# Diagonal products over 128 rows, both chunks of a unit in one matmul, with swapped head pairs in the second chunk

## The reference

```
A_cum = cumsum(A)                                   # within a chunk
Y_diag = einsum('bcshn,bczhn,bhcsz,bczhp->bcshp', C, B, exp(segsum(A)), X)
states = einsum('bcshn,bhcs,bcshp->bchpn', B, decay_states, X)
Y_off  = einsum('bcshn,bchpn,bhcs->bcshp', C, carried_states, exp(A_cum))
y = Y_diag + Y_off
```

## Time and profile before

| | |
|---|---|
| median of 3 runs | 679.62 us (677.96 to 679.92) |
| profiled execution | 678.2 us |
| its span | 676.5 us |
| busy share | TensorE 93%, VectorE 77%, ScalarE 57%, GpSimd 53% |
| mean granted TensorE clock | 0.969 |

### The profile page before, as it was taken

The page is one execution under the profiler, slowest core; times in us unless marked ns, Lnnn a source line. Parts: engine busy times, 40 slices in busy tenths (PEclk is TensorE's granted clock), DMA queues, the critical chain, the costliest instruction groups (busy, mean ns, idle before and its releaser), DMA issues.

```text
span 676.5 us, 21311 instructions
## 1 busy us (share of the span) xinstructions
PE 626.4 (93%) x8371; PEld 492.7 (73%) x8371; DVE 520.3 (77%) x947; ACT 383.4 (57%) x834; POOL 356.8 (53%) x416
## 2 busy tenths in 40 slices
PE   3597988999999999999999999999978989999995
PEld 2474766777777877777777777787867767888884
DVE  6599689888777887887788877778688366777766
ACT  3676544545647455655555564656664526665555
POOL 5674301636554453754634655447565646767652
PEclk9788888999999999999999999999997999999999
DMA  8654111152421231312122254222323744454411
GB/s 286 167 175 148 48 37 53 64 155 77 121 71 37 85 110 45 114 53 102 65 73 72 73 171 118 69 99 68 104 68 90 221 135 132 141 163 125 125 47 62
DMA packets 61914, 70.52 MB, mean 104 GB/s; under 512 B 13972, under 2 KB 33460, under 8 KB 61816
## 3 DMA queue, kind: packets, MB, share of 16 engines
q1 hardware_dynamic: 61816, 69.17, 32.5%
HBM read 54.45 MB, written 14.70 MB: 102 GB/s over the span
## 4 chain that ended last, share of the span: by engine, by line
PE 69%; DVE 13%; issue 5%; ACT 4%; DMA 3%; POOL 3%; SPq 1%; DVEq 0%; POOLq 0%; ACTq 0%
PE bank L1201 32%; PE bank L1968 11%; PE pair L1266 6%; PE bank L1210 4%; PE bank L2001 3%; DVE m_cv L1452 3%; PE pair L1239 3%; PE bank L1296 2%; PE bank L1219 2%; DMA p_wa_raw<-in_L_attn_in_proj_w_dram 2%; PE pair L1252 2%; DVE chain L594 1%; DVE chain L601 1%; DVE m_M L1482 1%; DMA h_lo_place<-y_scratch 1%
## 5 line engine op out<-in xcount | busy, mean ns | idle before, releaser
L1452 DVE SCALAR_TENSOR_TENSOR m_cv<-bank,gpc,m_cv 128x511 f32<-128x511 f32 (+2 forms) x192 | 143.4, 748 | 35.5 <-ACT m_cv L1359 30.9
L1201 PE MATMUL bank<-h_hi,w_hi 128*128 128x512 f32 x384 | 161.2, 420 | 4.7 <-DVE m_xs L1473 2.8
L1201 PE MATMUL bank<-h_lo,w_hi 128*128 128x512 f32 x384 | 153.1, 399 | 0.3 <-issue 0.3
L1201 PE MATMUL bank<-h_hi,w_lo 128*128 128x512 f32 x384 | 153.2, 399 | 0.0
L1597 POOL TENSOR_TENSOR m_S<-m_S,m_cd 128x128 f32<-128x128 f32 x96 | 40.0, 416 | 156.2 <-DVE m_S L1515 81.7
L1359 ACT ACTIVATE m_cv<-bank,gpc 128x512 f32<-128x512 f32 x96 | 72.0, 750 | 67.3 <-PE bank L1201 67.3
L1201 PEld LDWEIGHTS bank<-h_hi,w_hi 128*128 128x128 f32 x384 | 73.8, 192 | 24.4 <-issue 6.3
L1201 PEld LDWEIGHTS bank<-h_hi,w_lo 128*128 128x128 f32 x384 | 73.6, 192 | 17.4 <-issue 0.5
L1201 PEld LDWEIGHTS bank<-h_lo,w_hi 128*128 128x128 f32 x384 | 74.0, 193 | 13.6
L1371 ACT ACTIVATE m_M<-bank 128x512 f32<-128x512 f32 x128 | 76.2, 596 | 12.3 <-PE bank L1210 10.8
L1482 DVE TENSOR_TENSOR m_M<-m_M,pair 128x512 f32<-128x512 f32 x128 | 81.8, 680 | 0.2 <-issue 0.2
(11 more groups left out here) (184 smaller groups left out, 1271.9 us busy)
## 6 DMA issues: line engine op xcount, KB each, us to landing
m_ea<-ea_scratch SPq DMA_DIRECT2D x32, 256.0 KB
m_dd<-dd_scratch SPq DMA_DIRECT2D x32, 256.0 KB
y_scratch<-m_t SPq DMA_DIRECT2D x16, 512.0 KB, 3.3
h_lo_place<-y_scratch SPq DMA_DIRECT2D x16, 512.0 KB, 4.7
p_wm<-in_L_wmod_dram SPq DMA_DIRECT2D x6, 1024.0 KB, 7.1
m_wraw<-in_L_attn_in_proj_w_dram SPq DMA_DIRECT2D x18, 256.0 KB, 3.2
w_lo_place<-in_L_attn_input__dram SPq DMA_DIRECT2D x16, 256.0 KB, 4.9
out_dram<-t_o SPq DMA_DIRECT2D x16, 256.0 KB, 2.3
```

What stands on the lines that cost most here:

```text
L1201: ins = pe.matmul(A[k % 3][:, :], w[:, t, kc, :], h[:, n % NB, kc, :], start=(m == 0), stop=(m == 11))
L1452: ins = dve.scalar_tensor_tensor(out=cv[:, k % 3, lag:], in0=A[k % 3][:, 0:L - lag], scalar=s.gpc[:, gp, o:o + 1], in1=cv[:, k % 3, lag:], ...
```

## The change

A matmul of the diagonal now has all 128 rows: the tokens of both chunks. So that the two chunks don't add up, the second chunk works with the other head of the pair. The decay rows for chunk 1 are loaded from a second DRAM scratch in which the heads of each pair are swapped, and `placed` writes the second chunk of Xp and Xw to the swapped block. One matmul then gives head h of chunk 0 in one half of its 32 output partitions and head h^1 of chunk 1 in the other half. A unit has 16 diagonal matmuls in place of 32, and none accumulates.

The results go to columns 128 to 383 of the bank GB (OWN), beside the B transpose. For the partitions of odd heads the two chunks lie in order, for those of even heads they lie the other way round. ScalarE copies the even heads in the right order, with a 0/1 scale per partition (`even_heads`), VectorE adds the odd ones with a 0/1 scalar, GpSimd adds ScalarE's copy (`add_even`). New waits come with it, and `spread` and `weigh` become two instructions each. `head_parity` (GpSimd, once) makes the scales out of six small instructions. What counted y1_done for `sum_up` and `close` now counts y_added.

```diff
+        def store_both_orders(r, rows):
+            swapped = s.asw_d[r, rows2, :].rearrange("(x e) t -> x e t", e=2)
+            sp.dma_start(s.a_d[r, rows2, :], rows).then_inc(d_scr[pb], 16)
+            for e in range(2):
+                sp.dma_start(swapped[:, 1 - e, :], rows[e:P:2, :]).then_inc(d_scr[pb], 16)
+
         sp.wait_ge(a_act[pb], B_HI)
-        sp.dma_start(s.a_d[0, rows2, :], hi).then_inc(d_scr[pb], 16)
+        store_both_orders(0, hi)
         sp.wait_ge(a_v[pb], A_LO)
-        sp.dma_start(s.a_d[1, rows2, :], sums).then_inc(d_scr[pb], 16)
+        store_both_orders(1, sums)
...
+        def head_parity():
+
+            pool.wait_ge(konst, 10)
...
         M = sb("M", [P, 2, 2, HG * Q])
-        Xp, Xw = sb("Xp", [P, 2, 2 * HG, 32]), sb("Xw", [P, 2, HG * HD])
+        Xp, even0 = sb("Xp", [P, 2, 2 * HG, 32]), sb("even0", [P, 2, P])
         BTs = sb("BTs", [P, P])
         gate = sb("gate", [P, 2, L])
         S, S1 = sb("S", [P, 4, HG * HD]), sb("S1", [P, 2, HG * HD])
         t1 = sb("t1", [P, 2, L])
+        own_even, Xw = (even0, sb("even1", [P, 2, P])), sb("Xw", [P, 2 * HG, 2 * HD])
         s.Xp = Xp
         A, DB, XT, GB, YS = s.A, s.DB, s.XT, s.GB, s.pair
+        OWN = GB[:, P:3 * P].rearrange("p (q t) -> p q t", q=2)
 
...
+        def placed(t, c):
+
+            blocks = t[c * Q:(c + 1) * Q, :, :].rearrange("p (j a) (e d) -> p j (a e) d", a=2, e=2)
+            return blocks[:, :, 2:0:-1, :] if c else blocks[:, :, 0:4:3, :]
+
...
                     sp.dma_start(s.R[first:first + 2, u % 2, :, :].bitcast(F32).rearrange("r q (h s) -> r (q h) s", s=Q),
-                                 a_v[:, b, gp, :, chunk(u, c)]).then_inc(rl_ready[u % 2], 16)
+                                 a_v[c][:, b, gp, :, chunk(u, c)]).then_inc(rl_ready[u % 2], 16)
                 for r in range(2):
                     first = R_NEG + HG * r
-                    sp.dma_start(s.Lm[first:first + HG, u % 2, :, :].bitcast(F32),
-                                 na_v[r, b, gp, :, :, tok(u)]).then_inc(rl_ready[u % 2], 16)
+                    for c in range(2):
+                        sp.dma_start(s.Lm[first:first + HG, u % 2, :, c * Q:(c + 1) * Q].bitcast(F32),
+                                     na_v[c][r, b, gp, :, :, chunk(u, c)]).then_inc(rl_ready[u % 2], 16)
 
...
+                wait(pe, y1_done, u - 1)
                 pe.transpose(GB[:, 0:P], Bt[:, n % 2, tok(u)], s.ident[:, :]).then_inc(bt_done, 1)
...
-                        ins = pe.matmul(YS[group, c, 256:384], BTs[half, group], Xw[half, q, :], start=True, stop=True)
+                        ins = pe.matmul(YS[group, c, 256:384], BTs[half, group], placed(Xw, c)[:, 4 * q:4 * q + 4, :, :], start=True, stop=True)
...
             def diagonal(u):
 
                 wait(pe, y1_done, u)
+                pe.wait_ge(bt_read, min(u + 2, NU))
                 pe.wait_ge(s_new, n_new(u, 1))
                 pe.wait_ge(m_done, 2 * u + 2)
                 pe.wait_ge(xp_done, u + 1)
                 for q in range(2):
-                    for e in range(2):
+                    for a in range(2):
                         for j in range(4):
-                            for c in range(2):
-                                half, h = slice(64 * c, 64 * c + 64), 2 * j + e
-                                ins = pe.matmul(YS[32 * j:32 * j + 32, c, q * Q:(q + 1) * Q], Xp[half, u % 2, HG * q + h, :],
-                                                M[half, u % 2, q, h * Q:(h + 1) * Q], start=(e == 0), stop=(e == 1))
+                            h = 2 * j + a
+                            ins = pe.matmul(OWN[32 * j:32 * j + 32, q, (1 - a) * Q:(2 - a) * Q], Xp[:, u % 2, HG * q + h, :],
+                                            M[:, u % 2, q, h * Q:(h + 1) * Q], start=True, stop=True)
                 ins.then_inc(yd_done, 1)
...
-                out = Xp[:, u % 2, :, :].rearrange("p (j e) (m d) -> p j (e m) d", e=2, d=HD)[:, :, 0:4:3, :]
-                act.activation(out, XT[:, 0:2 * P].rearrange("p (j e d) -> p j e d", e=2, d=HD), ACT.Copy).then_inc(xp_done, 1)
+                for c in range(2):
+                    ins = act.activation(placed(Xp[:, u % 2, :, :], c), XT[c * Q:(c + 1) * Q, 0:2 * P].rearrange("p (j e d) -> p j e d", e=2, d=HD), ACT.Copy)
+                ins.then_inc(xp_done, 1)
+
+            def even_heads(u):
+
+                act.wait_ge(yd_done, u + 1)
+                wait(act, y_added, u - 1)
+                if u == 0:
+                    act.wait_ge(start.konst, start.PARITY)
+                act.activation(own_even[u % 2][:, :, :].rearrange("p q (c s) -> p q c s", c=2),
+                               OWN.rearrange("p q (c s) -> p q c s", c=2)[:, :, ::-1, :], ACT.Copy, scale=s.parity[:, 0:1]).then_inc(even_done, 1)
...
+                    if sl == 1 and v >= 0:
+                        even_heads(v)
...
-                first = 1 if i == 0 else 0
-                dst, scale = (v[:, n % 2, :, tok(u)].rearrange("p q (c s) -> p c q s", c=2) for v in (y1, ea))
-                own = YS[:, :, 0:P].rearrange("p c (q s) -> p c q s", q=2)
-                off = YS[:, :, P:2 * P].rearrange("p q (c s) -> p c q s", c=2)
+                first = Q if i == 0 else 0
+                dst, scale = (v[:, n % 2, :, tok(u)] for v in (y1, ea))
+                off, odd = YS[:, :, P:2 * P], s.parity[:, 1:2]
                 if i == 0:
                     dve.wait_ge(ea_ready[n % 2], 32 * (n // 2 + 1))
                     wait(dve, y_out, 2 * n - 2)
-                    dve.tensor_copy(dst[:, 0, :, :], own[:, 0, :, :])
-                dve.tensor_tensor(dst[:, first:, :, :], off[:, first:, :, :], scale[:, first:, :, :], ALU.mult).then_inc(yo_scaled, 1)
+                dve.tensor_tensor(dst[:, :, first:], off[:, :, first:], scale[:, :, first:], ALU.mult).then_inc(yo_scaled, 1)
+                if u == 0:
+                    dve.wait_ge(start.konst, start.PARITY)
+
+                dve.wait_ge(even_done, u + 1)
+                if i == 0:
+                    dve.tensor_scalar(dst[:, :, 0:Q], OWN[:, :, 0:Q], odd, None, ALU.mult)
                 dve.wait_ge(yo_scaled, u + 1)
-                dve.tensor_tensor(dst[:, first:, :, :], own[:, first:, :, :], dst[:, first:, :, :], ALU.add).then_inc(y1_done, 1)
+                dve.scalar_tensor_tensor(out=dst[:, :, first:], in0=OWN[:, :, first:], scalar=odd, in1=dst[:, :, first:],
+                                         op0=ALU.mult, op1=ALU.add).then_inc(y1_done, 1)
...
-                src = Xp[:, u % 2, :, :].rearrange("p (j e) (m d) -> p j (e m) d", e=2, d=HD)[:, :, 0:4:3, :]
                 w = s.wend[:, n // NB, n % NB, i, :].rearrange("p (j e) -> p j e", e=2).unsqueeze(3).broadcast_to([P, HG, 2, HD])
-                pool.tensor_tensor(Xw[:, :, :].rearrange("p q (j e d) -> p (q j) e d", e=2, d=HD), src, w, ALU.mult).then_inc(xw_done, 1)
+                for a in range(2):
+                    src, dst = (t[:, a::2, :].rearrange("p j (e d) -> p j e d", e=2) for t in (Xp[:, u % 2, :, :], Xw[:, :, :]))
+                    ins = pool.tensor_tensor(dst, src, w, ALU.mult)
+                ins.then_inc(xw_done, 1)
+
+            def add_even(u):
+
+                n = u // UPS
+                pool.wait_ge(y1_done, u + 1)
+                pool.wait_ge(even_done, u + 1)
+                y = y1[:, n % 2, :, tok(u)]
+                pool.tensor_tensor(y, y, own_even[u % 2][:, :, :], ALU.add).then_inc(y_added, 1)
...
-                    pool.wait_ge(y1_done, UPS * (n + 1))
+                    pool.wait_ge(y_added, UPS * (n + 1))
...
                     fade(v + 2, 0)
+                if v >= 0:
+                    add_even(v)
                 if v >= 4 and m == 0:
```

More of the change, by code:

```diff
@@ L235, in first_part @@
         d_scr, d_dd, h_lo, w_pool, zeroed, kcopy, we_ev)
+    start.picked = picked
+    start.konst, start.PARITY = konst, 16
     start.w_act, start.h_act, start.wt_pe, start.sec_pe, start.a_pe, start.d_gate, start.gpc_half = w_act, h_act, wt_pe, sec_pe, a_pe, d_gate, gpc_half
@@ L381, in gpsimd @@
                            base=0, pattern=[[-1, P]], channel_multiplier=1).then_inc(konst, 1)
-        pool.memset(scT[:, :, :], 0.0).then_inc(zero_sc, 1)
+        pool.memset(scT[:, :, :], 0.0).then_inc(picked, 1)
         pool.memset(pick[:, :], 0.0).then_inc(picked, 1)
         for k in range(KC):
-            pool.wait_ge(picked, k + 1)
+            pool.wait_ge(picked, k + 3)
             pool.affine_select(out=pick[:, :], in_=pick[:, :], compare_op=ALU.not_equal, fill=1.0,
                                base=-32 * k, pattern=[[-1, NB]], channel_multiplier=1).then_inc(picked, 1)
+        def head_parity():
+            pool.wait_ge(konst, 10)
+            pool.memset(parts[:, :], 1.0).then_inc(konst, 1)
+            pool.wait_ge(konst, 11)
+            pool.affine_select(out=parts[:, :], in_=parts[:, :], compare_op=ALU.is_ge, fill=0.0,
```

(15 more changed lines are left out.)

20 lines of the change are left out of this document (11 added, 9 removed).

## The result

| | before | after |
|---|---|---|
| median, beside each other on one chip | 678.79 us (677.13 to 679.92, 4 runs) | 706.09 us (704.91 to 707.43, 4 runs) |
| span of the profiled execution | 676.5 us | 705.4 us |

The changed kernel is slower, by a ratio of 1.0404, 95% interval 1.0375 to 1.0433. The forecast was 697, its range 688 to 710.

What follows compares the result with a forecast made beforehand. It took TensorE to bound nearly all of the main loop. Wait 30.9, saving -18.8, ScalarE 5.4 and GpSimd 1.0 sum to +18.5 us, on 678.2 giving 696.7; it said 697, range 688 to 710.

Steps and rivals of the forecast that it cites:

- The diagonal waits for ScalarE's copy of B: TensorE ahead of the diagonal: waits for the just-issued transpose's copy in 57 of 64 units, +30.9 us.
- a unit of the first kind: Unit without two weight transposes between B's transpose and the diagonal: 0.65 us of wait, 29 such units.
- The diagonal is shortened: TensorE's diagonal products: 0.46 us a unit instead of 0.79, saving 0.33 in 57 units, 18.8 us.
- its neighbours: Three measured matmul shapes used to price the 32 diagonal records: 0.50, 0.56 and 0.44 us.
- ScalarE's split `spread`: Second instruction priced at 0.26 us, delaying the exponent and TensorE's second decay product: 5.4 us, range 0 to 8.
- the odd units: Units where ScalarE also has a linear step ahead: 30 of 32 counted at 0.18 us added wait.
- `even_heads`, `weigh`, VectorE: Added ScalarE copy: nothing; doubled GpSimd weighing ahead of the states: 1 us in five units; VectorE: nothing.
- the rival's 13: Rival: `even_heads` 0.6 us late for VectorE in some 13 weight-copy units reaches TensorE, +8 us, 705; chance 0.10.
- The states, whose operand lies in pieces: Sign of being wrong: TensorE's states, streaming pieces of 16 elements, take over 0.22 us.
- DMA at 0 us, 2 at the outside: Six instead of four loads a unit, plus start work: loads have over a unit from request to use.
- The prediction's sign of being wrong: TensorE's clock falling in the loop because of the new gaps would show the forecast wrong.

Runs made afterwards that it cites:

- b_wait: Kernel before, with only the new wait added: the diagonal waits for ScalarE's copy of B issued just ahead; 695.36 us, 1.0245 of before.
- a_turnb: Changed kernel with the transpose of B moved ahead of the last slot's six projection matmuls; 694.75 us, 1.0236 of the kernel before.
- b_fourtiles: Kernel before, both chunks' diagonal products reading partitions 0 to 63, so as many matmuls on four tiles instead of eight; 693.46 us, 1.0209 of before.
- b_split: Kernel before, with only `spread` split into two instructions of 64 partitions each; 694.04 us, 1.0218 of before.
- a_bothsp: Changed kernel, exponent ahead of `spread`, B transpose ahead of six projection matmuls, SyncE requesting decay rows before y store and scales; 676.96 us, 0.9996 of before.
- a_sp: Changed kernel, only SyncE's order changed: decay rows requested ahead of the y store and scales; 704.47 us, 1.0388 of the kernel before.

## Why the prediction was right, and where its sizes were off

- **The diagonal waits for ScalarE's copy of B.** Right in mechanism and in count, 57; b_wait shows it alone and a_turnb its undoing. The size was forecast as 30.9 us and is 20.1. The start of 0.26 us behind the releaser was taken from a release by VectorE; behind ScalarE's copy it is 0.10, so a unit of the first kind costs 0.48 and not 0.65.
- **The diagonal is shortened.** It saves 14.9 us, not 18.8: 18.2 ns a record where I took 14.4 (0.46 us for 32), so 0.20 us in the usual unit and not 0.33, less than the 0.23 that the range allowed. The 14.9 also hold units in which the diagonals before took 0.9 us or more. The term was taken amid its neighbours, and the truth lies at the dear one, the off-diagonal products on four tiles with 17.5 ns. The Trainium skill (TensorEngine Tiling (Array Packing), "Tiling Modes") says that tiles of 32 columns work eight at a time with 64 rows and four with 128. b_fourtiles agrees with its direction; a full doubling would have left nothing of the saving, and the measured rates, 12.3 and 18.2 ns, leave a quarter of the diagonal's time as saving (1 - 18.2 / 24.6).
- **ScalarE's split `spread`.** The worst-sized term: 5.4 us forecast, at most 8 in the range, 16.2 measured, 14.4 in b_split. The step that failed is "I price it as a whole one: ScalarE's next instruction starts 0.26 us after it starts". It starts 0.78 us after the first half's start. The place, the odd units, was right.
- **`even_heads`, `weigh`, VectorE.** `even_heads` costs nothing that shows on TensorE; the trace has VectorE waiting for it for 7.0 us in 14 places, near the rival's 13, and TensorE's waits for VectorE did not grow by it (3.3 us ahead of the diagonal; before 5.8). `weigh` shows nothing here and 3.6 us once the holes are closed (a_bothsp). The states, whose operand lies in pieces, take their 0.22 us (320.54 to 320.76).
- **DMA at 0 us, 2 at the outside.** This term was wrong as argued: TensorE's matmuls wait 3.1 us for decay rows in 3 places. (The expectation of a_sp has 7.3 us in 7 places. That is a sum over matmuls and weight loads, which overlap.) That a load has over a unit from request to use is true only where SyncE isn't held up by a wait of its own. The pause costs more than its length where the clock falls behind it.
- **The clock.** The prediction's sign of being wrong, a fall of TensorE's clock in the loop behind a new gap, came for the 3.7 us from 151.40 on. The gap was that of the decay rows and not one of the foreseen ones: 57 waits of 0.2 to 0.4 us left the clock at 1.00 from 290 to 350 us.
- **Sum.** With the measured terms, 20.1 + 16.2 - 14.9 = 21.4 us of the loop's 26.9. Of the 5.5 left, 3.9 lie between the diagonal's end and the first decay, and they are those of the late decay rows: units 6, 10, 26 and 42 are longer there by 2.07, 0.65, 0.37 and 0.82 us. The other 1.6 lie elsewhere. With about 1.6 us that the slow records cost in the rest of unit 6 (1.3 of them inside the 16.2), the late rows stand for 3.9 + 1.6 = 5.5 us of the ledger; a_sp doesn't show that taking them away alone gives that back.

The forecast of 697 was 9 below the result: 10.8 too much on the wait, 3.9 too much on the saving and 10.8 too little on ScalarE, with 1.0 for `weigh` that doesn't show and the 5.5 that stand in none of its terms: -10.8 + 3.9 + 10.8 - 1.0 + 5.5 = +8.4 us. So it is partly luck that the result lies in the range: the two largest errors cancel, and three of the terms (the saving, ScalarE and, by the ledger, DMA) left the bounds that the prediction gave them. That b_wait and b_split alone make 14.4 and 14.9 us and the saving of 14.9 hardly lowers their sum of 29.3 (26.9) is in line with work that is waited out for VectorE, and with the late decay rows, which neither of the two has. How much is which, in the changed kernel, isn't shown.

## What to carry to other kernels

In this kernel, half the matmuls with twice the rows on half as many tiles in turn took three quarters of the time; price such a change by a measured rate at that number of tiles, and look at what a shared bank adds in waits before and behind. Splitting the short ScalarE copy by partitions cost its whole duration twice, not two strides, and that showed where another engine waited right behind. Where an in-order queue such as SyncE's has a wait in it, what stands behind inherits it: order requests by when they are wanted, and read a repair of one hole only after the others are closed.

## What the runs showed of the hardware

- ScalarE started the exponent 0.26 us behind the start of a copy of 128x256 that lasts 0.38 (306.49, 306.75). Two copies of 64 partitions and the same elements ran one after the other, 0.38 us each, and the exponent came behind the second's end (303.86, 304.64 in b_split).
- A diagonal released by ScalarE's copy started 0.10 us after the copy's end, one released by VectorE's mix 0.26; states released by GpSimd's `weigh` started 0.10 us after its end (159.45 + 1.20, 160.75 in a_sp).
- Records of small matmuls with 64 streamed columns came every 12.3 ns on eight tiles, 17.2 on four of 64 rows and 18.2 on four of 128 rows.
- Behind an idle TensorE of 1.82 us the granted clock was 0.54 for 3.7 us; between waits of 0.2 to 0.4 us in each unit it stayed at 1.00 (290 to 350 us).
